# Spacing the pair-weight scatters of a four-layer graph network kernel by a GpSimd counter operation

## The reference

```python
edge_index = jnp.stack([src, dst])
x = _layernorm(x + _L0_gnn_ref(...))   # mean of neighbours, 2 layers, 256 -> 512 -> 256
x = _layernorm(x + _L1_gnn_ref(...))   # 3 hops: H = A_w @ H @ Wn.T + H @ Ws.T + bias, elu between
x = _layernorm(x + _L2_gnn_ref(...))   # messages scaled by root degrees, leaky relu, row norm
x = _layernorm(x + _L3_gnn_ref(...))   # attention with 8 heads, softmax over a node's edges
```

## Time and profile before

| | |
|---|---|
| median of three runs | 2971.29 us (2961.16 to 2977.59) |
| profiled execution, span from first to last instruction | 2974.2 us |
| PE busy | 2470.6 us (83%) |
| DVE busy | 1396.0 us (47%) |
| POOL busy | 936.7 us (31%) |
| scatters (L794) | 416, 411.2 us busy, from 322.8 to 976.6 us |
| first product with a dense block (L1526) | 989.16 us |

### The profile page before, as it was taken

How to read it: one execution, slowest core, us unless ns; L and a number is a source line. 1 busy time by engine, 2 the same in 40 slices (tenths; PEclk the granted TensorE clock), 3 DMA queues, 4 the chain that set the end, 5 groups by cost and what they waited for, 6 DMA issues and landing times. The chain is left out here.

```text
span 2974.2 us, 32381 instructions
## 1 busy us (share of the span) xinstructions
PE 2470.6 (83%) x9483; PEld 1621.2 (55%) x9484; DVE 1396.0 (47%) x3940; ACT 707.2 (24%) x1552; POOL 936.7 (31%) x927
## 2 busy tenths in 40 slices
PE   3677789897987999999999999999977886457680
PEld 2444788343766555565556555577743444345560
DVE  7999656455665001030101001455575664546668
ACT  3776545111443000010001000255400000103112
POOL 0000256666666000000000000012167666576740
PEclk9888999998998999999999999999988998678885
DMA  6565678343344743444444434333558887646641
GB/s 233 243 253 225 212 238 264 118 138 97 112 121 137 152 151 129 151 134 151 129 152 133 151 119 145 93 106 102 113 168 271 278 282 245 209 132 190 192 127 43
DMA packets 209534, 493.89 MB, mean 166 GB/s; under 512 B 46457, under 2 KB 128430, under 8 KB 209134
## 3 DMA queue, kind: packets, MB, share of 16 engines
q1 hardware_dynamic: 135185, 301.30, 32.2%
q10 hardware_dynamic: 38173, 133.27, 12.8%
q0 software_dynamic: 36032, 57.60, 7.1%
HBM read 374.71 MB, written 117.32 MB: 165 GB/s over the span
## 5 line engine op out<-in xcount | busy, mean ns | idle before, releaser
L794 POOL DMA_INDIRECT table_dense_weights<-pair_weight,dst x416 | 411.2, 988 | 563.5 <-DVE weights_c L849 324.8
L1526 PE MATMUL banks<-own_term,features_and_rows 128*128 128x391 f32 (+1 forms) x1656 | 552.3, 491 | 0.0
L2134 POOL DMA_INDIRECT features_and_rows<-table_heads,src x376 | 401.7, 1068 | 191.4 <-issue 107.9
L1526 PEld LDWEIGHTS banks<-own_term,features_and_rows 128*128 128x128 f32 x1656 | 312.2, 189 | 226.8
L1552 DVE TENSOR_SCALAR features_and_rows<-banks,hop_bias 128x391 f32<-128x391 f32 (+1 forms) x24 | 15.0, 625 | 762.2 <-PE banks L1526 762.2
L954 PE MATMUL banks<-split_rows,count_columns 128*128 128x512 f32 x1200 | 322.1, 415 | 19.6 <-issue 12.6
L2531 PE MATMUL banks<-features_and_rows,edge_to_window 128*128 x880 | 233.4, 427 | 104.5 <-DVE edge_to_window L2492 71.6
L1526 PE MATMUL banks<-features_and_rows 128*128 128x391 f32 (+1 forms) x840 | 282.4, 491 | 0.0
L954 PEld LDWEIGHTS banks<-split_rows,count_columns 128*128 128x128 f32 x1200 | 226.3, 193 | 76.8 <-issue 21.7
L2531 PEld LDWEIGHTS banks<-features_and_rows,edge_to_window 128*128 128x128 f32 x880 | 181.3, 210 | 156.5 <-issue 122.5
L558 PE MATMUL banks<-features_and_rows,pair_and_bias_rows 128*128 128x400 f16 x806 | 184.3, 388 | 87.1 <-DVE features_and_rows L540 51.9
(11 more groups left out here) (425 smaller groups left out, 3016.8 us busy)
## 6 DMA issues: line engine op xcount, KB each, us to landing
hidden<-table_counts SPq DMA_DIRECT2D x305, 160.0 KB
table_dense_weights<-weights_c ACTq DMA_DIRECT2D x26, 1600.0 KB, 5.7
own_term<-table_dense_weights SPq DMA_DIRECT2D x52, 782.0 KB
features_and_rows<-table_rows_by_edge SPq DMA_DIRECT2D x58, 528.0 KB
own_term<-table_dense_weights SPq DMA_DIRECT2D x34, 780.5 KB
pair_and_bias_rows<-table_edge_rows ACTq DMA_DIRECT2D x50, 512.0 KB
weights_c<-table_edge_rows ACTq DMA_DIRECT2D x50, 512.0 KB
table_rows_by_edge<-features_and_rows SPq DMA_DIRECT2D x48, 528.0 KB
```

Of the source, the lines that this page charges most:

```text
L794: e.indirect_dma_start(out=self.table, out_offset=bass.IndirectOffsetOnAxis(ap=self.place[:, t:t + 1], axis=0), in_=self.values[:, t:t + 1 ...
L1526: m = e.matmul(psum[b][:, 0:wide], z_block(block)[:, f * P:(f + 1) * P], streamed[tile % STREAM][:, lo - from_column:lo - from_column + wi ...
L2134: e.indirect_dma_start(out=to[:, k, :], out_offset=None, in_=t_h, in_offset=bass.IndirectOffsetOnAxis(ap=src[:, t:t + 1], axis=0)).then_in ...
```

## The change

`multiplied_beside` and all its calls go. Behind each scatter GpSimd gets an `iota` that writes 128 counting integers per partition to a spare buffer, and that waits for the `iota` before it. Nothing reads the buffer. The waits on register values are written with a mask (`& 511`) into a second register instead of `snap` with bounds, and `step % 32` becomes `step & 31`.

```diff
+PAUSE = 128
+        spare_count = sb("spare_count", [P, PAUSE], I32)
+        def wait_loaded(e, sem, loaded, bound):
+            e.reg_alu(bound, loaded, 511, ALU.bitwise_and)
+            e.wait_ge(sem, bound)
+        s_paused, paused = pr.sem("pause_done"), [0]
+        def pause(e):
+            if paused[0]:
+                e.wait_ge(s_paused, paused[0])
+            e.iota(spare_count[:, :], [[1, PAUSE]], base=0, channel_multiplier=0).then_inc(s_paused, 1)
+            paused[0] += 1
...
-                e.wait_ge(s_zeroed, e.snap(regs[2 * n + 1], min_val=3, max_val=WINDOWS + 2))
+                wait_loaded(e, s_zeroed, regs[2 * n + 1], bound)
...
-                e.wait_ge(s_built, e.snap(regs[v % ROTATING], min_val=1, max_val=BUILD_STEPS))
+                wait_loaded(e, s_built, regs[v % ROTATING], bound)
...
-            def tiles(self, e, s, c, half_step=0):
-                for i, k in enumerate(range(c, UNROLL, 3) if s < THIRDS else range(c, UNROLL, 2)):
+            def tiles(self, e, s, c):
+                for k in range(c, UNROLL, 3) if s < THIRDS else range(c, UNROLL, 2):
                     t = s * UNROLL + k
-                    if i == 2:
-                        multiplied_beside(e, half_step, 1)
                     self.count[c][s % 2] += 16
                     e.indirect_dma_start(...).then_inc(self.landed[c][s % 2], 16)
+                    pause(e)
...
             def step(self, e, s):
-                multiplied_beside(e, 2 * s)
-                self.tiles(e, s, 0, 2 * s)
+                self.tiles(e, s, 0)
                 if s > 1:
                     self.in_memory(e, s - 2)
                 if s:
-                    multiplied_beside(e, 2 * s + 1)
-                    self.rest(e, s - 1, 2 * s + 1)
+                    self.rest(e, s - 1)
...
-        def multiplied_beside(e, half_step, half=0):
-            if IN_ROWS <= half_step < IN_LAYERS:
-                e.wait_ge(s_a_used, min(45 + 4 * (half_step - IN_ROWS) + 2 * half, of_group(Q1, 0) + NODE_TILES * COUNT_GROUPS - 1))
-            elif IN_LAYERS <= half_step < IN_SECOND:
-                e.wait_ge(pr.done["pe"], dense_layers_from[0] + max(1, 6 * (half_step - IN_LAYERS) - 10 + 3 * half))
-            elif IN_SECOND <= half_step < IN_TURNS:
-                e.wait_ge(s_a_used, min(of_group(Q2, 0) + 4 * (half_step - IN_SECOND) + 2 * half, of_group(Q3, 0) - 1))
-            elif IN_TURNS <= half_step < IN_HOPS:
-                e.wait_ge(pr.done["pe"], turned_from[0] + K_IN * (NODE_TILES // 2 + 10 * (half_step - IN_TURNS)))
-            elif half_step >= IN_HOPS:
-                e.wait_ge(s_z_made, 3 * (half_step - IN_HOPS) + 1 + half)
...
-                        e.wait_ge(weights.steps, e.snap(reg, min_val=1, max_val=STEPS))
+                        wait_loaded(e, weights.steps, reg, stream_register[1])
...
-                    e.wait_ge(s_begun, step % 32)
+                    e.wait_ge(s_begun, step & 31)
...
-                e.wait_ge(s_mm, e.snap(ends_of_node[d], min_val=1, max_val=MERGE_STEPS + UNROLL))
+                wait_loaded(e, s_mm, ends_of_node[d], bound)
```

More of the change, by code:

```diff
@@ L547, in build_pe @@
             pe_regs.extend(e.alloc_register(f"step_{k}") for k in range(2 * REGS_AT_ONCE))
-            regs = pe_regs
+            regs, bound = pe_regs, e.alloc_register("zeroed_windows")
             for s in range(BUILD_STEPS):
@@ L565, in build_act @@
             regs = [e.alloc_register(f"window_end_{k}") for k in range(ROTATING)]
+            bound = e.alloc_register("window_end_step")
             for b in [RUN_BANK, RUN_BANK + 1, *range(ROTATING)]:
@@ L795, in tiles, with rest @@
                                          in_=self.values[:, t:t + 1], in_offset=None).then_inc(self.landed[c][s % 2], 16)
-            def rest(self, e, s, half_step=0):
+                    pause(e)
+            def rest(self, e, s):
                 e.wait_ge(self.landed[0][s % 2], self.count[0][s % 2])
-                self.tiles(e, s, 1, half_step)
+                self.tiles(e, s, 1)
                 if s < THIRDS:
@@ L822, in end @@
                 self.in_memory(e, STEPS - 1)
-        dense_layers_from, turned_from = [0], [0]
-        IN_ROWS, IN_LAYERS, IN_SECOND, IN_TURNS, IN_HOPS = 8, 29, 66, 99, 101
-        def multiplied_beside(e, half_step, half=0):
-            if IN_ROWS <= half_step < IN_LAYERS:
-                e.wait_ge(s_a_used, min(45 + 4 * (half_step - IN_ROWS) + 2 * half, of_group(Q1, 0) + NODE_TILES * COUNT_GROUPS - 1))
-            elif IN_LAYERS <= half_step < IN_SECOND:
-                e.wait_ge(pr.done["pe"], dense_layers_from[0] + max(1, 6 * (half_step - IN_LAYERS) - 10 + 3 * half))
-            elif IN_SECOND <= half_step < IN_TURNS:
-                e.wait_ge(s_a_used, min(of_group(Q2, 0) + 4 * (half_step - IN_SECOND) + 2 * half, of_group(Q3, 0) - 1))
-            elif IN_TURNS <= half_step < IN_HOPS:
-                e.wait_ge(pr.done["pe"], turned_from[0] + K_IN * (NODE_TILES // 2 + 10 * (half_step - IN_TURNS)))
-            elif half_step >= IN_HOPS:
-                e.wait_ge(s_z_made, 3 * (half_step - IN_HOPS) + 1 + half)
         weights = Scatter("weights", t_dense, place_i, pair_weight)
@@ L1220, in from_hidden @@
                                               split_of[j], xb)
-        dense_layers_from[0] = pr.count[pr.done["pe"].name]
         to_hidden(0)
@@ L1309, in residual_gnn @@
         V(lambda e: e.reciprocal(rdeg[:, :], rdeg[:, :]), d2)
-        turned_from[0] = pr.count[pr.done["pe"].name]
         in_groups(turn0)
@@ L1619, in hops_sp @@
                     e.wait_ge(*ready)
-                stream_register.append(e.alloc_register("weight_steps_in_memory"))
+                stream_register.extend((e.alloc_register("weight_steps_in_memory"), e.alloc_register("weight_steps_awaited")))
             reg = stream_register[0]
@@ L2537, in merge_act @@
             ends_of_node = [e.alloc_register(f"node_end{k}") for k in range(NODE_TILES)]
+            bound = e.alloc_register("node_end_step")
             e.load(ends_of_node, merge_control[0:1, MERGE_STEPS:MERGE_STEPS + NODE_TILES])
```

## The result

| | median us | lowest to highest | runs |
|---|---|---|---|
| before | 2972.08 | 2961.16 to 2977.59 | 4 |
| with the change | 3088.25 | 3085.61 to 3095.34 | 4 |

The ratio is 1.0399, 95% interval 1.0372 to 1.0426: the change makes the kernel 116 us slower here. The forecast was 2971 us, with a range of 2953 to 2996.

The account below looks back on a forecast made before the run. TensorE was taken to bound the kernel, with VectorE setting the build's pace and scatters off the path by some 110 us. Four terms of 0 left 2974.2 us of span, 2971 us as median; range 2953 to 2996.

Parts of the forecast that it names:

- Part 1: GpSimd's scatters: removing the conditions on TensorE's progress frees GpSimd time but gains 0 on the path.
- part 3: Neighbours of the scatters: competition with count loads and counter writes beside VectorE, taken as 0, with ends of +27 and -27.
- Rival 4: Counter hides in the gap between scatters; they run at 1.29 us, end near 876; 2971 us, sharing the forecast's 0.66.
- The pace: GpSimd's scatter loop: a counter adds 0.30 us, giving 1.59 us per scatter against 1.51 before.
- Part 2: The 416 added counter operations on GpSimd: scatters end near 1001 us, off the path, cost 0.
- Rival 1: Ahead of blocks 24 and 25: counters cost much more than their row, 46 us at 0.66 added, 3017 us; chance 0.11.
- the 1105 us of the prediction: Dense blocks: latest issue of the last scatter before TensorE waits, reached at 0.55 us added per scatter.
- Rival 3: VectorE held up by the counter writes: 17 us if all is on the path, 2988 us; chance 0.08.
- Rival 2: Even spacing helps the count loads, shrinking ScalarE's 27.0 us of DMA waits: about 20 us gain, 2951 us; chance 0.15.
- most of the 133.2 us: GpSimd's scatters: share of this idle time, beyond first pair sums and plain issue, put down to TensorE's conditions.
- 15 more and not 25: Between 949 and 989 us: about 25 more scatters would fall in and behind this busy DMA stretch, hidden by early loads.
- Part 4: Register edits: 8 us on TensorE's sequencer and 4 on ScalarE's in the build, hidden by VectorE; merge 0, at most -5.

Follow-up runs that it names:

- e3: Kernel before with the register edits, no counters, conditions on TensorE's progress kept everywhere but in the dense layers; 3118.47 us, ratio 1.0431.
- e4: Kernel before with the register edits alone, its conditions kept and no counters; 2994.77 us, ratio 1.0018.
- e1: Changed kernel without its 416 counter operations, so scatters run with neither counters nor conditions; 3205.43 us, ratio 1.0713.
- f1: The changed kernel itself, unedited, run again on chip 7; 2800.77 us, ratio 0.9998 to the kernel before there.
- e2: Changed kernel with the conditions on TensorE's progress put back and the counters kept; 2990.94 us, ratio 1.0002.
- e6: Changed kernel with two counter operations behind each scatter where it has one; 2913.42 us, ratio 1.0399, on chip 12.
- e7: Changed kernel with eight counters in a row at the head of each step of eight scatters, none between scatters; 2822.55 us, ratio 1.0073.
- the first comparison: The changed kernel against the kernel before, four runs each, on a chip not recorded; 3088.25 against 2972.08 us, ratio 1.0399.
- group 1: First follow-up runs, on chip 14: variants of counters, conditions and register edits against the kernel before at 2990.28 us; ratios 1.0002 to 1.0713.
- e5: Kernel before with the register edits, conditions replaced by counters in the dense layers only; 2802.49 us, ratio 1.0001, on chip 12.

## Why the prediction was wrong

**The step that failed** is the price of the neighbours. Part 1 says of the places where the conditions stood "No other engine waits in these places, so the gain on the path is 0", and part 3 weighs only transfers against transfers: "At an equal mean pace I leave this at 0, with ends of +27 and -27." Rival 4 saw the scatters come closer together and found "no price" for it. The price is TensorE's own issue. On the slower kind, long runs of scatters go with a state of one instruction or a few per 0.7-us tick: +130 us in the layers alone at 1.27 us a scatter (337 in e3 against 207 in e4), +89 and +69 us in the passes at 1.43, of which 16.7 us in the second are the late count load. The conditions had been a closed loop: GpSimd stopped whenever TensorE was behind. That these breaks matter is shown by e3 against e4; whether they end the state or keep it from setting in, no run shows. The median distance of two scatters went up with the change (1.264 to 1.425 us), but the distances over 1.9 us fell from 57 to 8, and the last but one of these began at 404 us. A mean pace was the wrong quantity. The same step missed a gain: in the layers, TensorE's idle time put down to issue fell from 17.5 to 0.5 us, and the stage is 28 us shorter.

The rows had a hint. In the earlier trace rows TensorE stood idle 13.4 and 19.6 us; the prediction quotes the 3.1 and 6.9 us for ScalarE and passes over the rest, which the same rows put down to issue: 10.2 and 12.6 us. On the bounding engine, "issue" in the middle of a loop of products is a question and not an answer. Nothing in that trace gave its price without breaks, though: that took e1 and e3.

**Which parts held.**
- The pace: 0.26 us for a counter (forecast 0.23), 0.16 us added to the pitch (forecast 0.30, bounds 0 to 0.53), last scatter at 965 us (forecast 1001, bounds 876 to 1097). The Trainium skill, page Perfetto Trace Analysis, section GPSIMD Engine Instruction, asks for start-to-start spacing instead of spans; the trace agrees that the span misleads, 0.26 us of span against 0.16 us of pitch, since the gap ahead of the next scatter falls from 0.30 to 0.17 us when a counter stands there.
- Part 2's cost of 0: f1 (0.9998) shows it, and e2 (1.0002) agrees in its total, though not stage by stage. Rival 1 has the right mechanism and did not come about; e6 and e7 show it with its price. On the faster chips, where the hops start at 893 us instead of 989, the last scatter costs nothing at 963 us, 21.7 us at 1011 and 102.9 us at 1099. So the limit lies between 963 and about 990 us there; the 1105 us of the prediction belongs to hops that start 96 us later, which would be 1009 here, so it was some 20 us too late.
- Rival 3: VectorE's two operations take 427 and 324 ns with the counters (413 and 292 before; 409 and 292 in e1 without them). That is (14 + 32) x 25 = 1.2 us in all. The Trainium skill, page SBUF — State Buffer, section "Who interferes with whom", has GpSimd and VectorE shut each other out only where VectorE takes both of its ports, which its pace does not show here. The trace agrees for most of the operations but not for all: the median of the 324-ns group is 286 ns with and without counters, but its longest takes 526 ns, for 380 before and 347 in e1, so single ones are held up beside a counter.
- Rival 2: no gain of this kind from even spacing. ScalarE's waits for loads into `hidden` grew from 22.1 to 37.7 us, 20.7 us of them the late load.
- Two of its figures are loose, without effect on the time. The "most of the 133.2 us" for TensorE's conditions is 71.6 us, the sum of the rows that name TensorE in the scatters' view of before. And from 949 to 1001 us a distance of 1.59 us gives 33 scatters where there were 18, so 15 more and not 25.
- Part 4: the build is busy 195.25 and 258.99 us for 194.65 and 259.54; e4 agrees.

**Is "the same" right elsewhere?** On chip 7 it was (0.9998). That is no excuse: the trace read was of a slower chip, and the loss was to be found on that kind.

**What stays open.** Why there are two kinds of runs, and whether the chip or the hour decides; what the tick of 0.70 to 0.74 us is, and what it looks at; whether it is a late supply of instructions; whether it takes indirect DMAs or any unbroken GpSimd work to set it off; which break is long enough. My theory before the runs, that each scatter blocks TensorE's issue while it lasts, is refuted by e3's grid and its 21 us behind the last scatter. What stands is that the state came in the first comparison and in group 1 alone, and there depended on how the scatters were spaced. The runs narrow the rest a little. It is not GpSimd's busy share: in e1's layers it is 189.56 of 289 us and TensorE ticks, in the changed kernel's 153.76 of 176 us and TensorE runs full. It is not the load on the DMA engines (e3: 7%). A pitch of 1.43 us is enough in the layers (174 us on either kind of chip), where TensorE needs 175.27 / 430 = 0.41 us for a product, and not in the passes, where f1 needs 0.12 us (19.99 / 165) and 0.24 us (148 / 625); that this is because the passes issue more instructions per microsecond is argued, not shown. That the second pass took 213 us in e2 and 172 in e4 is unexplained; TensorE's idle time there is 16.5 us for 9.2 by issue and 21.2 for 10.0 by ScalarE. A version that keeps the conditions in the passes and has counters in the layers (e5) could gain there on the slower chips by these numbers (174 for 202 us), but e2's second pass warns against counting on it; it was only run where all versions are equal.

## What to carry to other kernels

Before taking away a wait that looks idle, ask what it keeps apart: a condition on another engine's progress is a brake that works only when that engine is behind, and the one fixed delay tried on the slower kind, 0.16 us more from scatter to scatter, did the same in the layers but not in the passes. Idle time put down to issue on the bounding engine is to be priced in the prediction, by an end of the range as wide as that engine's share of the stage. And read the time of the kernel before, in each group of runs, before reading a ratio: an experiment on a chip that lacks the effect says nothing about its cause.

## What the runs showed of the hardware

- The same kernel can take two times, and each of the chips met showed one of them: the kernel before takes 2990 us on chip 14 (and 2972 on one not recorded) and 2802 to 2806 on four others. For the changed kernel the build (279 us) and the dense blocks (927.0 us in both traces) are alike; the 288 us between the two spans (3087.9 and 2799.9) arise only in stretches in which GpSimd issues many indirect DMAs: 210 up to the first dense block, 43 between dense blocks and merge, 35 in the merge.
- The part between dense blocks and merge shows in the kernel before too. Products beside the gathers there (2193 to 2533 us), first in the trace of before, then in f1:

```profile
L2237 PE MATMUL banks<-edge_to_window,edge_weight 104*128 104x512 f32 (+1 forms) x224 | 123.1, 634 | 53.2 <-DVE edge_to_window L2311 32.1 <-issue 21.1
```

```profile
L2234 PE MATMUL banks<-edge_to_window,edge_weight 104*128 104x512 f32 (+1 forms) x224 | 111.4, 579 | 0.2 <-DVE edge_to_window L2308 0.2
```

- On the slower kind TensorE's issue can fall to one instruction per 0.7, 1.4 or 2.1 us, at a granted clock of 0.50 (1.2 GHz); in e3 the grid of these ticks has nothing of GpSimd's pitch (1.266 us), and it outlived the last scatter by 21 us. Such idle time is shown as "issue", but not all that is shown so is this: the merge has 146.5 us of it in f1 and 152.5 in the kernel before.
- Right around the last scatter the DMA engines can be 79% to 97% busy for 15 to 20 us at 19 to 31 GB/s, on either kind of chip (before, changed kernel, f1).
